# Graph and feed-forward layers on one core: five one-hot rows of each sort group moved to ScalarE

## The chip, the cores and the metric

One core of a Trainium2 chip runs the whole program. The metric is the device time of one execution in microseconds; the number given is the median of three runs. The profile is of a single execution. TensorE multiplies, VectorE, ScalarE and GpSimd do the elementwise work, and DMA queues move data.

## The reference

Four layers, each of a graph network and a feed-forward part, are applied to 384 nodes with 512 features, over 12,288 edges. The change touches the first step of layer 0's graph part only:

```python
def _L0_gnn_ref(x, edges, Wv, bv, Ww, bw, Wa, ba, gamma, beta):
    out = (x @ Wv + bv).reshape(n, H, HD).transpose(1, 0, 2)
    x1, x2 = x[edges[0]], x[edges[1]]
    e = jnp.concatenate([x1, x2], axis=1) @ Ww + bw
    e = e.reshape(-1, H, 2 * HD).transpose(1, 0, 2)
    w = (leaky_relu(e, 0.01) @ Wa + ba)[..., 0]
    mat = full((H, n, n), -inf).at[:, edges[0], edges[1]].set(w)
    y = jnp.matmul(nan_to_num(softmax(mat)), out).transpose(1, 0, 2)
    return layernorm(elu(y).reshape(n, HID) + x) * gamma + beta
...
x = x + _L0_gnn_ref(_layernorm(x), edge_index, ...)
...
x = x + _L3_ffn_ref(_layernorm(x)[None], ...)
```

The kernel multiplies the node features by `Ww` once per node (384 rows instead of 12,288) and gathers the products of an edge's two nodes with one-hot matrices, tile by tile of 128 edges. For that each tile must hold edges of one pair of chunks of 128 nodes, so the edges are sorted into such buckets first.

## The kernel before, in words

The edges lie as 128 partitions x 96 columns (`ET` = 96). For every edge VectorE works out its place in the sorted order, split into a column `q_f` and a row `r_f`, and a key `slo1` that holds both of its node numbers. Sorting is then matrix multiplication: for each of the 96 columns t, a one-hot row matrix `slot_one` (1 where the index equals `q_f[:, t]`) and a matrix `spread` (the key where the index equals `r_f[:, t]`, else 0) are multiplied on TensorE, and all 96 products are summed in the bank `sortk`. Both matrices are 128x128, a "row" of the group in what follows.

The columns go in 12 groups of 8 (`UN`), with two buffers for each kind. A group has 16 such rows. In the kernel before, GpSimd makes 7 of the 8 `slot_one` rows (`POOLED`, line 1153) and VectorE makes the eighth (line 1290) and all 8 spreads (line 1291). Before group g an engine waits on `sort_used` until TensorE has consumed group g-2. TensorE waits for `slot_hot` and `spread_made` of its group.

Between the groups stands other work of TensorE: 12 "units", 128x512 products of the node features with the weights `L0_gnn_Ww`. Four matmuls make a unit; units 6 to 11 have a fifth, the bias row. Units 0 and 1 come first, then

```python
AFTER_GROUP = {1: 2, 2: 3, 4: 4, 5: 5, 7: 6, 8: 7, 10: 8, 11: 9}
SPLIT_AFTER = {0: 0, 1: 1, 3: 2, 4: 3, 6: 4, 7: 5, 9: 6, 10: 7, 11: 8}
```

say behind which group TensorE computes which unit, and behind which group's rows VectorE splits which unit. Units 10 and 11 follow the sort. Each unit u is split into three bf16 parts: ScalarE copies the upper part from PSUM (`top_part`, line 1051), VectorE subtracts it (line 1250), ScalarE copies the middle part (line 1058), and VectorE subtracts again for the lower part (line 1244); it also multiplies and reduces the unit (lines 1253, 1258). In ScalarE's program the copies stand in the order top 0, top 1, middle 0, top 2, middle 1 and so on, and nothing else lies between them in this stage. After group 2's rows VectorE also works out the tiles' chunks (`tile_chunks`).

When `sortk` is full VectorE decodes the keys, TensorE transposes them, and the tile loop over 104 tiles starts once the last unit's parts are made (`parts_made`). GpSimd, when it has made its rows of group 11, writes 20 columns of records to `tab_bucketed` by indirect DMA. The program's order is written out by hand for each engine; there is no scheduler. All of TensorE's matmuls have line 373, a helper's.

Of the kernel before, what the change touches and what calls it, by code (L numbers as in the profile page):

```python
# [11 lines left out]
P = 128  # L12
# [5 lines left out]
ET = E // P  # L18
# [14 lines left out]
UN = 8  # L33
# [129 lines left out]
def gnn_ffn_program(nc, A, out):  # L163
    ctx = ExitStack()
    with ctx:
# [3 lines left out]
        def sem(name):  # L169
            return ctx.enter_context(nc.semaphore(name))  # L170
# [65 lines left out]
        def view(off, *shape):  # L236
            n = 1
            for s in shape:
                n *= s
            assert off + n <= AW, (off, n)  # L240
            v = arena[:, off:off + n]
            if len(shape) == 2:
                v = v.rearrange("p (a b) -> p a b", a=shape[0])
            elif len(shape) == 3:
                v = v.rearrange("p (a b c) -> p a b c", a=shape[0], b=shape[1])
            return v
# [44 lines left out]
        def few_underway(pool, q, earlier, most):  # L291

            if q >= most:
                k = q - most
                pool.wait_ge(ranks_landed[k % UN], 16 * (earlier + k // UN + 1))
        bucketed_loaded = sem("bucketed_loaded")
        bucketed_cleared = sem("bucketed_cleared")
        factor_ready = sem("factor_ready")
# [481 lines left out]
        def flat(a):  # L780
            return a[:].rearrange("p t n -> p (t n)")
# [7 lines left out]
        ew_in = view(tail + 3 * ET, ET)  # L789

        slot5 = ring.slot(5).rearrange("p c n -> p (c n)")
        spread = slot6.rearrange("p (b t r) -> p b t r", b=2, t=UN)
        slot_one = slot7.rearrange("p (b t q) -> p b t q", b=2, t=UN)
        left_f = slot5[:, 0:1024].rearrange("p (b n) -> p b n", b=2)
# [17 lines left out]
        prod_l = slot5[:, 1024:2048].rearrange("p (b h d) -> p b h d", b=2, h=4)  # L812
        s0 = ST * H8
        cs_e, cd_e, slo1, dlo1, q_f, r_f, tmp_e = (xs[:, s0 + k * ET:s0 + (k + 1) * ET] for k in range(7))
        hot9 = flat(cnt_dst)[:, 0:NBK * ET].rearrange("p (k t) -> p k t", k=NBK)
        before9 = flat(mask_dst)[:, 0:NBK * ET].rearrange("p (k t) -> p k t", k=NBK)
        past8 = flat(cnt_dst)[:, 0:ST * 8].rearrange("p (q k) -> p q k", k=8)
# [40 lines left out]
        def unit_part(u, k):  # L858
            r, q, t = UNITS[u]
            return parts0[:, r, t, k, q * 512:q * 512 + 512]  # L860
# [35 lines left out]
        def _(pe, o):  # L896
# [22 lines left out]
            for g in range(ET // UN):  # L919
                pe.wait_ge(slot_hot, g + 1)  # L920
                pe.wait_ge(spread_made, g + 1)
                for j in range(UN):
                    t = UN * g + j
                    last = mm(sk[:, 0:P], slot_one[:, g % 2, j, :], spread[:, g % 2, j, :], t == 0, t == ET - 1)
                last.then_inc(sort_used if g < ET // UN - 1 else banks.full_of("sortk"), 1)
                if g in AFTER_GROUP:
                    if banks.at == sort_bank:
                        banks.at = (sort_bank + 1) % NB
                    unit(AFTER_GROUP[g])
# [114 lines left out]
        @on("act")  # L1044
        def _(act, o):
            act_norm(act, NORM["l0"])
            act_transposed(act, "l0x", xT)

            def top_part(u):
                b = banks.filled(act, unit_name(u))  # L1050
                nc.scalar.activation(unit_part(u, 0), b, ACT.Copy).then_inc(hi_made, 1)

            top_part(0)
            for u in range(len(UNITS)):
                if u + 1 < len(UNITS):
                    top_part(u + 1)
                act.wait_ge(pieces_made, u + 1)
                nc.scalar.activation(unit_part(u, 1), left_f[:, u % 2, :], ACT.Copy).then_inc(bf16_made, 1)
            act.wait_ge(sorted_cleared, 16)

            def eight(i, ahead):
                for b in range(UN):
                    j = b // TB
                    if b % TB == 1 and j < ahead:
                        act.wait_ge(hot_made, 2 * i + j + 2)
                        act.nop(nofuse=True)
                        load_keys(act, 2 * i + j + 3, 1 - j)

                    act.wait_ge(z_free, UN * i + b + 3)
                    for h in range(H8 // 2, H8):  # L1070
                        last = nc.scalar.activation(prod2[:, b % 2, h, :], prod2[:, b % 2, h, :], ACT.Copy, accum_out=w_sum[:, b, h:h + 1])  # L1071
                    last.then_inc(heads_summed, 1)

            act.wait_ge(hot_made, 1)
            load_keys(act, 2)
            FULL = (SB - 3) // 2
            with act.Fori(0, FULL) as i:
                eight(i, 2)
            for i in range(FULL, ST // UN):
                eight(i, min(2, max(0, SB - 3 - 2 * i)))  # L1080

            def head_exp(h, t):
                return nc.scalar.activation(weights_of(h, t), wm[t].rearrange("p (j h) -> p h j", h=H8)[:, h, :], ACT.Exp,
                                            bias=gate[:, 5, t * H8 + h:t * H8 + h + 1])

            def head_transposed(h):
                act_copy(act, f"l0p{h}{NT - 1}", pwT[h % 2][:, NT - 1, :], N)

            nc.scalar.activation(gate[:, 15, 41:42], eps_col[:], ACT.Exp)
            act.wait_ge(neg_max, 1)  # L1090
            for h in range(H8):
                head_exp(h, 0)
            nc.scalar.activation(ost[:, :, :, HD], ones[:, 0:NT * H8].rearrange("p (t h) -> p t h", t=NT), ACT.Copy)
            for t in range(NT):
                b = banks.filled(act, f"l0o{t}")
                nc.scalar.activation(ost[:, t, :, 0:HD], b.rearrange("p (h d) -> p h d", h=H8),
                                     ACT.Copy).then_inc(banks.free_of(f"l0o{t}"), 1)
            act.wait_ge(totals_ready, 1)
            for c in range(NT):
                act_copy(act, f"cnt{c}", cnt_src[:, c, :], N)  # L1100
            act.wait_ge(neg_max, NT)
            for h in range(H8):
                if h >= 2:
                    banks.filled(act, f"l0p{h - 2}{NT - 1}")
                head_exp(h, 1)
                head_exp(h, 2).then_inc(exp_done, 1)
                if h >= 1:
                    if h >= 3:
                        banks.filled(act, f"l0y{h - 3}")
                    head_transposed(h - 1)  # L1110
                if h == 6:
                    elu_part_exp(act, 0)
            banks.filled(act, f"l0y{H8 - 3}")
            head_transposed(H8 - 1)
            elu_part_exp(act, 1)
            elu_part_exp(act, 2)
            act.wait_ge(node_base, 1)
            for c in range(NT):
                act_copy(act, f"cntT{c}", cnt_dst[:, c, :], N)
            for n, (step, t) in enumerate(ROWS0):  # L1120
                act_row_std(act, n, t)
                if step == 3:
                    act.wait_ge(row_ready, 2 * t + 2)
                    nc.scalar.activation(xn2[:, t, :], xn[:, t, :], ACT.Copy, scale=rstd[:, t:t + 1]).then_inc(again_ready, 1)
# [20 lines left out]
        def _(pool, op):  # L1145

            pool.wait_ge(slot_ready, 1)
            for g in range(ET // UN):
                if g >= 2:
                    pool.wait_ge(sort_used, g - 1)  # L1150
                for j in range(POOLED):
                    t = UN * g + j
                    last = nc.gpsimd.tensor_scalar(slot_one[:, g % 2, j, :], iota[:, 0:P], q_f[:, t:t + 1], None, ALU.is_equal)
                last.then_inc(slot_hot, 1)
# [26 lines left out]
        def _(dve, od):  # L1181
# [53 lines left out]
            V.scalar_tensor_tensor(out=pos[:], in0=r_f, scalar=float(ST), in1=q_f, op0=ALU.mult, op1=ALU.add).then_inc(pos_ready, 1)  # L1235

            od.link(V.scalar_tensor_tensor(out=slo1, in0=dlo1, scalar=KEY_BASE, in1=slo1, op0=ALU.mult, op1=ALU.add))
            dve.wait_ge(params, PARAMS)
            wa_bc = wa.unsqueeze(1).broadcast_to([P, 4, P])
            V.tensor_scalar(wa99, wa, 1.0 - 0.01, None, ALU.mult)  # L1240
# [43 lines left out]
            for g in range(ET // UN):  # L1284
                if g >= 2:
                    dve.wait_ge(sort_used, g - 1)
                for j in range(UN):
                    t = UN * g + j
                    if j >= POOLED:
                        V.tensor_scalar(slot_one[:, g % 2, j, :], iota[:, 0:P], q_f[:, t:t + 1], None, ALU.is_equal)  # L1290
                    last = V.tensor_scalar(spread[:, g % 2, j, :], iota[:, 0:P], r_f[:, t:t + 1], slo1[:, t:t + 1],
                                           ALU.is_equal, ALU.mult)
                last.then_inc(spread_made, 1)
                if g == 2:
                    tile_chunks()
                if g in SPLIT_AFTER:
                    split_unit(SPLIT_AFTER[g])
# [1995 lines left out]
```

## Time and profile before

| | us |
|---|---|
| median of 3 runs | 1792.34 |
| lowest and highest run | 1790.09, 1795.05 |
| profiled execution, its own time | 1795.19 |
| its span in the profile | 1793.4 |
| TensorE busy | 1601.0 |
| VectorE busy | 881.6 |
| GpSimd busy | 642.0 |
| ScalarE busy | 501.5 |
| sort stage, first unit to the end of unit 11 | 17.56 to 99.21 |

The span is the time between the profile's first and last event; the execution's own time is slightly longer. "Busy" is the time in which an engine computes. "PEclk" is the clock granted to TensorE as a share of its full 2.4 GHz, so 0.50 is 1.2 GHz. In a timeline a row is one instruction or several like it in a row (xN), and its bracket gives the idle time of the engine just before it and what ended that. Neighbouring instructions on an engine overlap a little, so the distance of starts can be smaller than a duration.

### The profile page before, as it was taken

The numbers are of one execution on the slowest core, as the hardware profiler recorded it, in microseconds if no ns is written. First come the engines' busy times: TensorE is split into PE (matmuls) and PEld (weight loads), VectorE is DVE, ScalarE is ACT, GpSimd is POOL, SyncE is SP. The second block draws the span as 40 slices with busy tenths as digits, with TensorE's granted clock in tenths as the row PEclk, the third lists the DMA queues.
The fourth block names the chain that finished last, engine by engine and source line by source line (L and its number), as shares of the span: only waits on it lengthen the run. The fifth ranks groups of instructions, "written<-read, shape, count | busy, mean of one in ns | idle before, by whom it ended". The sixth has DMA issues, their size and how long they took to land. (4 is left out here: it accounts for less than half of the span.)

```text
span 1793.4 us, 22802 instructions
## 1 busy us (share of the span) xinstructions
PE 1601.0 (89%) x6910; PEld 888.4 (50%) x6940; DVE 881.6 (49%) x2161; ACT 501.5 (28%) x1586; POOL 642.0 (36%) x756
## 2 busy tenths in 40 slices
PE   6989999998697999999996877589799999999798
PEld 3534444446444645555553645334344555555555
DVE  8878888878644343344354154598623101111322
ACT  1134444447431413223231124311200111111234
POOL 5868787873332333333341713556300000000000
PEclk9989999999698999999997887589799999999899
DMA  8030101005413223122316744445326121220020
GB/s 313 2 102 25 60 25 60 25 8 133 124 48 127 78 82 90 57 81 63 94 42 135 255 138 140 138 133 160 118 71 216 51 91 52 99 67 16 9 62 18
DMA packets 119611, 161.71 MB, mean 90 GB/s; under 512 B 49497, under 2 KB 61721, under 8 KB 119154
## 3 DMA queue, kind: packets, MB, share of 16 engines
q1 hardware_dynamic: 93056, 115.43, 20.6%
q0 software_dynamic: 18592, 29.91, 6.1%
q10 hardware_dynamic: 7890, 15.44, 2.6%
q8 instruction: 41, 0.67, 0.2%
q14 instruction: 32, 0.26, 0.1%
HBM read 145.26 MB, written 15.47 MB: 90 GB/s over the span
## 5 line engine op out<-in xcount | busy, mean ns | idle before, releaser
L373 PE MATMUL psum<-arena 128*128 128x384 f32 (+9 forms) x1804 | 319.8, 333 | 33.0 <-issue 13.3
L373 PE MATMUL psum<-arena,ring 128*128 (+1 forms) x1478 | 323.2, 364 | 9.0 <-issue 6.3
L373 PE MATMUL psum<-xT,ring 128*128 128x384 f32 x928 | 317.5, 503 | 10.4 <-ACT ring L3118 4.5
L373 PEld LDWEIGHTS psum<-arena 128*128 128x128 f32 (+5 forms) x1804 | 197.3, 155 | 162.8 <-issue 88.3
L373 PE MATMUL psum<-ring,arena 128*128 128x512 f32 (+1 forms) x570 | 261.9, 607 | 8.6 <-DVE ring L663 3.9
L373 PE MATMUL psum<-ring,xT 128*128 128x512 f32 x552 | 253.9, 613 | 2.1 <-DMA bc<-in_wide 0.8
L373 PEld LDWEIGHTS psum<-xT,ring 128*128 128x128 f32 x928 | 181.5, 197 | 139.9 <-issue 28.3
L373 PEld LDWEIGHTS psum<-arena,ring 128*128 128x128 bf16 (+1 forms) x1504 | 139.7, 115 | 130.3 <-issue 29.0
L1071 ACT ACTIVATE ring<-ring 128x128 f32<-128x128 f32 x416 | 123.3, 297 | 173.6 <-DVE ring L1357 164.6
L373 PEld LDWEIGHTS psum<-ring,xT 128*128 128x128 f32 x552 | 106.0, 197 | 125.4 <-issue 121.6
L373 PEld LDWEIGHTS psum<-ring,arena 128*128 128x128 f32 (+1 forms) x570 | 99.7, 188 | 131.3 <-issue 130.2
L851 POOL DMA_INDIRECT tab_bucketed<-rec,pos x96 | 95.7, 997 | 190.0 <-DMA tab_bucketed<-rec,pos 182.4
L2144 POOL DMA_INDIRECT tab_sorted<-rec,pos x104 | 100.0, 962 | 173.2 <-DMA tab_sorted<-rec,pos 151.1
L1357 DVE SCALAR_TENSOR_TENSOR ring<-psum,wa 128x1024 f32<-128x1024 f32 x104 | 127.3, 1224 | 61.4 <-PE psum L373 60.5
L1165 POOL TENSOR_SCALAR arena<-iota,arena 128x128 bf16<-128x128 f32 x200 | 121.6, 616 | 16.8 <-DVE xT L1371 13.9
L1177 POOL DMA_INDIRECT tab_w<-xT,pair x104 | 109.8, 1056 | 48.8 <-DMA tab_w<-xT,pair 31.9
L408 ACT ACTIVATE arena<-psum 128x384 f32<-128x384 f32 (+1 forms) x130 | 61.9, 498 | 182.8 <-PE psum L373 157.6
L482 ACT ACTIVATE std<-mv,eps_col 128x1 f32<-128x1 f32 x57 | 16.8, 294 | 220.9 <-DVE mv L465 217.9
L1071 ACT ACTIVATION_READ_ACCUMULATOR ring<-ring 128x1 f32 x416 | 77.5, 186 | 0.0
L624 POOL DMA_INDIRECT ring<-tab_h,sd_t x61 | 62.6, 1026 | 37.1 <-issue 13.3
L2071 DVE TENSOR_TENSOR xn<-xn,psum 128x512 f32<-128x512 f32 x24 | 16.5, 687 | 118.7 <-PE psum L373 118.5
L1365 DVE TENSOR_REDUCE mask_dst<-ring 128x4 f32<-128x512 f32 x104 | 70.2, 675 | 0.0
(478 smaller groups left out, 1667.3 us busy)
## 6 DMA issues: line engine op xcount, KB each, us to landing
ring<-in_L_ffn_w SPq DMA_DIRECT2D x22, 1024.0 KB, 6.8
ring<-in_L_gnn_m_w SPq DMA_DIRECT2D x8, 1024.0 KB, 6.0
ring<-in_L_ffn_expert_weights SPq DMA_DIRECT2D x8, 1024.0 KB
ring<-tab_key ACTq DMA_DIRECT2D x24, 256.0 KB
ring<-in_L_gnn_Wv SPq DMA_DIRECT2D x5, 1024.0 KB, 5.1
tab_w<-xn SPq DMA_DIRECT2D x6, 768.0 KB, 14.7
ring<-in_L_gnn_Ww SPq DMA_DIRECT2D x4, 1024.0 KB
ring<-in_L_gnn_wq SPq DMA_DIRECT2D x4, 1024.0 KB
```

The lines of the kernel that those rows point to most:

```text
L373: return nc.tensor.matmul(o, a, b, start=start, stop=stop)
L408: nc.scalar.activation(dst, b[:, 0:w], ACT.Copy).then_inc(banks.free_of(name), 1)
L482: nc.scalar.activation(std[:, t:t + 1], mv[:, t, 1:2], ACT.Sqrt, bias=eps_col[:, 0:1]).then_inc(row_std, 1)
L624: return nc.gpsimd.indirect_dma_start(o, None, table, bass.IndirectOffsetOnAxis(ap=column.bitcast(U32), axis=0), **more)
L851: nc.gpsimd.indirect_dma_start(tab_bucketed, bass.IndirectOffsetOnAxis(ap=pos[:, q:q + 1].bitcast(U32), axis=0), rec[:, q, :], None).then_ ...
L1071: last = nc.scalar.activation(prod2[:, b % 2, h, :], prod2[:, b % 2, h, :], ACT.Copy, accum_out=w_sum[:, b, h:h + 1])
L1165: last = nc.gpsimd.tensor_scalar(edge_is[:, j, k, s_, :], iota[:, 0:P], key_rq[:, s_, T:T + 1], None, ALU.is_equal)
L1177: nc.gpsimd.indirect_dma_start(tab_w, bass.IndirectOffsetOnAxis(ap=pair[:, q:q + 1].bitcast(U32), axis=0), w_edge0[:, q, :], None).then_in ...
L1357: V.scalar_tensor_tensor(out=prod2[:, b % 2], in0=z_bank[:, b % 2], scalar=0.0, in1=wa_all, op0=ALU.max, op1=ALU.mult).then_inc(z_free, 1)
L1365: V.tensor_reduce(w_sum[:, b, 0:H8 // 2], prod2[:, b % 2, 0:H8 // 2, :], AX, ALU.add).then_inc(halves_summed, 1)
L2071: V.tensor_tensor(xn2[:, t, :], xn2[:, t, :], b, ALU.add).then_inc(banks.free_of(f"{tag}{t}"), 1)
L2144: nc.gpsimd.indirect_dma_start(tab_sorted, bass.IndirectOffsetOnAxis(ap=pos2[:, q:q + 1].bitcast(U32), axis=0), rec[:, q, :], None).then_i ...
```

## The change

Of the 16 rows of a group, five move to ScalarE, which makes each in two activations. With `ACT_SLOTS` = 3, GpSimd no longer makes the `slot_one` rows 0 to 2 of a group (4 are left), and with `ACT_SPREADS` = 2, VectorE no longer makes the spreads 0 and 1 (6 are left, and its one slot row). ScalarE first computes the distance |index - place| for the five into a new double buffer `apart`, waits on `apart_made` for its own results, then computes ReLU(1 - distance) for slot rows, and ReLU(key - key x distance) for spreads. VectorE provides `key_less`, the negated key, in one more instruction (`keys_ready`). TensorE waits for one more semaphore a group, `act_hot`. ScalarE's copies of the units keep their order among themselves, and stand behind the groups as in `SPLIT_AFTER`.

```diff
--- before.py
+++ after.py
@@ -293,6 +293,9 @@
             if q >= most:
                 k = q - most
                 pool.wait_ge(ranks_landed[k % UN], 16 * (earlier + k // UN + 1))
+        apart_made = sem("apart_made")
+        act_hot = sem("act_hot")
+        keys_ready = sem("keys_ready")
         bucketed_loaded = sem("bucketed_loaded")
         bucketed_cleared = sem("bucketed_cleared")
         factor_ready = sem("factor_ready")
@@ -789,6 +792,7 @@
         ew_in = view(tail + 3 * ET, ET)
 
         slot5 = ring.slot(5).rearrange("p c n -> p (c n)")
+        ACT_SLOTS, ACT_SPREADS = 3, 2
         spread = slot6.rearrange("p (b t r) -> p b t r", b=2, t=UN)
         slot_one = slot7.rearrange("p (b t q) -> p b t q", b=2, t=UN)
         left_f = slot5[:, 0:1024].rearrange("p (b n) -> p b n", b=2)
@@ -812,6 +816,8 @@
         prod_l = slot5[:, 1024:2048].rearrange("p (b h d) -> p b h d", b=2, h=4)
         s0 = ST * H8
         cs_e, cd_e, slo1, dlo1, q_f, r_f, tmp_e = (xs[:, s0 + k * ET:s0 + (k + 1) * ET] for k in range(7))
+        key_less = cs_e
+        apart = view(e0, 2, ACT_SLOTS + ACT_SPREADS, P)
         hot9 = flat(cnt_dst)[:, 0:NBK * ET].rearrange("p (k t) -> p k t", k=NBK)
         before9 = flat(mask_dst)[:, 0:NBK * ET].rearrange("p (k t) -> p k t", k=NBK)
         past8 = flat(cnt_dst)[:, 0:ST * 8].rearrange("p (q k) -> p q k", k=8)
@@ -919,6 +925,7 @@
             for g in range(ET // UN):
                 pe.wait_ge(slot_hot, g + 1)
                 pe.wait_ge(spread_made, g + 1)
+                pe.wait_ge(act_hot, g + 1)
                 for j in range(UN):
                     t = UN * g + j
                     last = mm(sk[:, 0:P], slot_one[:, g % 2, j, :], spread[:, g % 2, j, :], t == 0, t == ET - 1)
@@ -1050,12 +1057,35 @@
                 b = banks.filled(act, unit_name(u))
                 nc.scalar.activation(unit_part(u, 0), b, ACT.Copy).then_inc(hi_made, 1)
 
-            top_part(0)
-            for u in range(len(UNITS)):
+            def middle_part(u):
                 if u + 1 < len(UNITS):
                     top_part(u + 1)
                 act.wait_ge(pieces_made, u + 1)
                 nc.scalar.activation(unit_part(u, 1), left_f[:, u % 2, :], ACT.Copy).then_inc(bf16_made, 1)
+
+            top_part(0)
+            act.wait_ge(keys_ready, 1)
+            for g in range(ET // UN):
+                if g >= 2:
+                    act.wait_ge(sort_used, g - 1)
+                rows = [(r_f, UN * g + j) for j in range(ACT_SPREADS)] + [(q_f, UN * g + j) for j in range(ACT_SLOTS)]
+                for k, (at, t) in enumerate(rows):
+                    last = nc.scalar.activation(apart[:, g % 2, k, :], iota[:, 0:P], ACT.Abs, bias=at[:, t:t + 1], scale=-1.0)
+                last.then_inc(apart_made, 1)
+                act.wait_ge(apart_made, g + 1)
+                for k, (at, t) in enumerate(rows):
+                    j = t % UN
+                    if k < ACT_SPREADS:
+                        nc.scalar.activation(spread[:, g % 2, j, :], apart[:, g % 2, k, :], ACT.Relu, bias=slo1[:, t:t + 1],
+                                             scale=key_less[:, t:t + 1])
+                    else:
+                        last = nc.scalar.activation(slot_one[:, g % 2, j, :], apart[:, g % 2, k, :], ACT.Relu, bias=ones[:, 0:1],
+                                                    scale=-1.0)
+                last.then_inc(act_hot, 1)
+                if g in SPLIT_AFTER:
+                    middle_part(SPLIT_AFTER[g])
+            for u in range(len(SPLIT_AFTER), len(UNITS)):
+                middle_part(u)
             act.wait_ge(sorted_cleared, 16)
 
             def eight(i, ahead):
@@ -1148,7 +1178,7 @@
             for g in range(ET // UN):
                 if g >= 2:
                     pool.wait_ge(sort_used, g - 1)
-                for j in range(POOLED):
+                for j in range(ACT_SLOTS, POOLED):
                     t = UN * g + j
                     last = nc.gpsimd.tensor_scalar(slot_one[:, g % 2, j, :], iota[:, 0:P], q_f[:, t:t + 1], None, ALU.is_equal)
                 last.then_inc(slot_hot, 1)
@@ -1235,6 +1265,7 @@
             V.scalar_tensor_tensor(out=pos[:], in0=r_f, scalar=float(ST), in1=q_f, op0=ALU.mult, op1=ALU.add).then_inc(pos_ready, 1)
 
             od.link(V.scalar_tensor_tensor(out=slo1, in0=dlo1, scalar=KEY_BASE, in1=slo1, op0=ALU.mult, op1=ALU.add))
+            V.tensor_scalar(key_less, slo1, -1.0, None, ALU.mult).then_inc(keys_ready, 1)
             dve.wait_ge(params, PARAMS)
             wa_bc = wa.unsqueeze(1).broadcast_to([P, 4, P])
             V.tensor_scalar(wa99, wa, 1.0 - 0.01, None, ALU.mult)
@@ -1288,8 +1319,9 @@
                     t = UN * g + j
                     if j >= POOLED:
                         V.tensor_scalar(slot_one[:, g % 2, j, :], iota[:, 0:P], q_f[:, t:t + 1], None, ALU.is_equal)
-                    last = V.tensor_scalar(spread[:, g % 2, j, :], iota[:, 0:P], r_f[:, t:t + 1], slo1[:, t:t + 1],
-                                           ALU.is_equal, ALU.mult)
+                    if j >= ACT_SPREADS:
+                        last = V.tensor_scalar(spread[:, g % 2, j, :], iota[:, 0:P], r_f[:, t:t + 1], slo1[:, t:t + 1],
+                                               ALU.is_equal, ALU.mult)
                 last.then_inc(spread_made, 1)
                 if g == 2:
                     tile_chunks()
```

Line numbers of the changed kernel are some 3 to 32 higher. On ScalarE, from its last copy of the transposed features to the copies that follow group 3, the order was this before the change (`xT`, `arena` and `ring` hold the features, the units' parts and the buffers; line 1051 is the upper part of units 0, 1, 2 and 3, line 1058 the middle part of units 0, 1 and 2):

```order
L408 ACTIVATE xT<-psum 128x384 [waits bank_full3]
L1051 ACTIVATE arena<-psum 128x512 [waits bank_full5]
L1051 ACTIVATE arena<-psum 128x512 [waits bank_full6]
L1058 ACTIVATE arena<-ring 128x512 [waits pieces_made]
L1051 ACTIVATE arena<-psum 128x512 [waits bank_full0]
L1058 ACTIVATE arena<-ring 128x512 [waits pieces_made]
L1051 ACTIVATE arena<-psum 128x512 [waits bank_full1]
L1058 ACTIVATE arena<-ring 128x512 [waits pieces_made]
```

In the changed program it is this, from the rows of group 1 on (line 1073 is the distances, 1079 the spreads, 1082 the slot rows, 1058 and 1064 the upper and middle parts):

```order
L1073 ACTIVATE arena<-iota,xT 128x128 x5
L1079 ACTIVATE ring<-arena,xT 128x128 [waits apart_made]
L1079 ACTIVATE ring<-arena,xT 128x128
L1082 ACTIVATE ring<-arena,ones 128x128 x3
L1058 ACTIVATE arena<-psum 128x512 [waits bank_full0]
L1064 ACTIVATE arena<-ring 128x512 [waits pieces_made]
L1073 ACTIVATE arena<-iota,xT 128x128 [waits sort_used]
L1073 ACTIVATE arena<-iota,xT 128x128 x4
L1079 ACTIVATE ring<-arena,xT 128x128 [waits apart_made]
L1079 ACTIVATE ring<-arena,xT 128x128
L1082 ACTIVATE ring<-arena,ones 128x128 x3
```

Between group 1's rows and group 2's stand the copy of unit 2's upper part, which waits until TensorE has filled its bank (`bank_full0`), and the middle part of unit 1. The same pair stands between groups 3 and 4, 4 and 5, and so on.

TensorE's own order is unchanged. In the changed program its first groups read so; the 128x128 rows are groups 1 to 4, the 128x512 rows units 2 and 3:

```order
L376 MATMUL psum<-ring 128x128 [waits act_hot,spread_made,slot_hot]
L376 MATMUL psum<-ring 128x128 x7
L376 MATMUL psum<-ring,xT 128x512 [waits bank_free0]
L376 MATMUL psum<-ring,xT 128x512 x3
L376 MATMUL psum<-ring 128x128 [waits act_hot,spread_made,slot_hot]
L376 MATMUL psum<-ring 128x128 x7
L376 MATMUL psum<-ring,xT 128x512 [waits bank_free1,slot_arrived1]
L376 MATMUL psum<-ring,xT 128x512 x3
L376 MATMUL psum<-ring 128x128 [waits act_hot,spread_made,slot_hot]
L376 MATMUL psum<-ring 128x128 x7
L376 MATMUL psum<-ring 128x128 [waits act_hot,spread_made,slot_hot]
L376 MATMUL psum<-ring 128x128 x7
```

What is new there is the wait for `act_hot` at the head of each group.

## Rows read from the trace of the kernel before

**Rows 1.** Page: TensorE's busy time, share, instructions; the chain's shares of the span by engine.
```profile
PE 1601.0 (89%) x6910; PEld 888.4 (50%) x6940; DVE 881.6 (49%) x2161; ACT 501.5 (28%) x1586; POOL 642.0 (36%) x756
...
PE 30%; DVE 3%; issue 1%; ACT 1%; DMA 0%; POOL 0%; another core or an unknown queue 0%; ACTq 0%; DVEq 0%
```

**Rows 2.** Windows: length, busy us per engine, PEclk, DMA share, GB/s; sort stage, tile loop.
```profile
40.00:60.00 20.00, 17.34 (x74) 10.88 (x73) 19.46 (x57) 2.23 (x4) 17.79 (x27) 0.91 0.00 1
60.00:80.00 20.00, 20.00 (x105) 13.14 (x105) 18.07 (x50) 3.35 (x6) 16.89 (x30) 1.00 0.00 1
120.00:140.00 20.00, 19.30 (x118) 9.49 (x117) 16.43 (x47) 8.95 (x56) 14.84 (x20) 1.00 0.09 29
```

**Rows 3.** Timeline, TensorE, sort stage: start us, us, instruction [idle before <-releaser].
```profile
27.21 2.05 PE L373 MATMUL psum<-ring 128*128 128x128 f32 x16 [0.26 <-POOL ring L1153]
31.26 2.79 PE L373 MATMUL psum<-ring 128*128 128x128 f32 x16 [1.99 <-POOL ring L1153]
33.84 4.57 PE L373 MATMUL psum<-ring,xT 128*128 128x512 f32 x8
38.24 1.95 PE L373 MATMUL psum<-ring 128*128 128x128 f32 x16
40.03 3.60 PE L373 MATMUL psum<-ring,xT 128*128 128x512 f32 x8
...
48.07 2.50 PE L373 MATMUL psum<-ring 128*128 128x128 f32 x16 [2.65 <-DVE ring L1291]
50.36 4.84 PE L373 MATMUL psum<-ring,xT 128*128 128x512 f32 x8
...
73.83 1.12 PE L373 MATMUL psum<-rows,ones 1*128 1x512 f32 x2
```

**Rows 4.** Timeline of ScalarE, sort stage.
```profile
23.55 0.60 ACT L1051 ACTIVATE arena<-psum 128x512 bf16<-128x512 f32 x1 [9.93 <-PE psum L373]
...
55.24 0.60 ACT L1051 ACTIVATE arena<-psum 128x512 bf16<-128x512 f32 x1 [10.46 <-PE psum L373]
55.73 0.62 ACT L1058 ACTIVATE arena<-ring 128x512 bf16<-128x512 f32 x1
```

**Rows 5.** Timeline of VectorE, sort stage: rows of group 4.
```profile
45.35 1.99 DVE L1291 TENSOR_SCALAR ring<-iota,xT 128x128 f32<-128x128 f32 x7
...
47.46 0.46 DVE L1291 TENSOR_SCALAR ring<-iota,xT 128x128 f32<-128x128 f32 x1
```

**Rows 6.** Timeline of GpSimd, sort stage: rows of groups 0 to 6.
```profile
22.88 32.00 POOL L1153 TENSOR_SCALAR ring<-iota,xT 128x128 f32<-128x128 f32 x49 [18.01 <-DVE xT L1232]
```

**Rows 7.** Groups by form, ScalarE, whole span: busy us, mean ns | idle before.
```profile
L1071 ACT ACTIVATE ring<-ring 128x128 f32<-128x128 f32 x416 | 123.3, 297 | 173.6 <-DVE ring L1357 164.6 <-issue 9.0
...
L408 ACT ACTIVATE arena<-psum 128x384 f32<-128x384 f32 x124 | 58.3, 494 | 170.4 <-PE psum L373 145.2 <-PE psum L2273 20.8 <-PE psum L2281 3.6
...
L1973 ACT ACTIVATE arena<-psum,packed 128x384 f32<-128x384 f32 x48 | 27.8, 580 | 98.8 <-PE psum L373 98.8
...
L1051 ACT ACTIVATE arena<-psum 128x512 bf16<-128x512 f32 x12 | 7.2, 597 | 73.9 <-PE psum L373 73.9
...
L1124 ACT ACTIVATE xn<-xn,rstd 128x512 f32<-128x512 f32 x3 | 2.2, 721 | 3.7 <-DVE rstd L1535 3.7
```

**Rows 8.** Timeline of ScalarE, tile loop.
```profile
112.06 0.29 ACT L1071 ACTIVATE ring<-ring 128x128 f32<-128x128 f32 x1
...
112.26 0.19 ACT L1071 ACTIVATION_READ_ACCUMULATOR ring<-ring 128x1 f32 x1
```

**Rows 9.** Windows, columns as in rows 2: behind two stops, and the tile loop's start.
```profile
33.00:35.00 2.00, 2.00 (x7) 1.48 (x7) 2.00 (x7) 0.00 (x0) 2.00 (x4) 0.50 1.02 427
50.00:52.00 2.00, 2.00 (x5) 1.04 (x5) 2.00 (x7) 0.00 (x0) 2.00 (x5) 0.50 0.00 0
105.00:110.00 5.00, 5.00 (x16) 2.02 (x17) 0.17 (x1) 0.00 (x0) 3.84 (x4) 0.50 0.04 5
110.00:111.00 1.00, 1.00 (x5) 0.41 (x3) 0.51 (x1) 0.00 (x0) 0.00 (x0) 0.56 0.03 2
```

## The prediction

> **What bounds the kernel now.** I read the page first: TensorE is busy in 89% of the span, every other engine in half of it or less, and the chain of waits is TensorE for 30 of the 35% that it covers [rows 1]. The chain does not reach back to the sort stage, so I took that stage from the windows: TensorE computes in 17.34 of 20 us in one and in all 20 of the next, while VectorE works 19.46 and 18.07, GpSimd 17.79 and 16.89 and ScalarE 2.23 and 3.35 [rows 2]. Then I read each engine's timeline there, looking for the starts that have an idle time and a releaser in brackets. From 27 us on, TensorE stands twice: 1.99 us before group 1, for GpSimd, and 2.65 us before group 4, for VectorE [rows 3]. Elsewhere its groups and units follow each other without a gap. So the rows of the one-hot matrices bound the stage only there, 4.6 us in all, and TensorE bounds the rest.
>
> Each of these two stops costs more than its length. A group takes 1.95 us and a unit 3.60 us at full speed; behind the stops they take 2.79 and 4.57, and 2.50 and 4.84 [rows 3]. That is 1.81 us and 1.79 us more. The granted clock in those stretches is 0.50, the 1.2 GHz level, against 1.00, 2.4 GHz, before [rows 9].
>
> ScalarE is idle for most of the stage, but look at what ends its idle times: each of its copies of a unit's upper part starts 0.04 us after TensorE ends that unit (50.36 + 4.84 = 55.20, the copy at 55.24), after 10.46 us of waiting [rows 3, 4]. It is free in time, but it stands at a place in its program.
>
> **What the change removes.** GpSimd makes four rows a group instead of seven, at 32.00 / 49 = 0.65 us each [rows 6]: 2.0 us less. VectorE makes six spreads instead of eight, at 1.99 / 7 = 0.28 us [rows 5]: 0.57 us less. At best this takes away both stops and their slow stretches: 4.6 + 3.6 = 8.2 us. No DMA is added or moved, on no queue.
>
> **What it adds.** VectorE's one more multiplication, over 96 elements, costs no more than a 128-element row at 0.28 us [rows 5] and runs ahead of the first group beside units 0 and 1: nothing on the path. On ScalarE it adds ten activations a group. Their kind is not in the trace; I build it from the nearest rows. A 128x128 ACTIVATE lasts 0.297 us, and the next instruction starts 0.20 us after it did (112.06, 112.26) [rows 7, 8]. A bias column makes 128x384 cost 580 instead of 494 ns, so +0.09; a scale column makes 128x512 cost 721 instead of 597 ns, so +0.12 [rows 7]. Eight activations with a bias column at 0.29, two with both at 0.41, and 0.1 at the end of each half, whose last result is waited for, give 3.3 us a group. The lower bound is copies without columns, 2.2 us; the upper bound ten at 0.41 and as much for the waits, 4.3 us. I take 3.3, since both column costs are seen. The Trainium skill (ScalarE: Activation LUTs, What ACT_TABLE_LOAD costs) prices each pointer operand at about 93 ns; an estimate from that page gives 3.1 us, which would make the sum below 1.6 us smaller.
>
> **What is queued behind what.** This decides. ScalarE's program now runs: rows of group g, then (after groups 0, 1, 3, 4, 6, 7, 9, 10, 11) the copy of the *next* unit's upper part, which waits for TensorE to finish that unit, then the middle part, and only then the rows of group g+1. But TensorE takes the unit after group g and group g+1 directly behind the unit. Where both stand in that order, ScalarE cannot start group g+1 before TensorE has ended the unit, and TensorE then waits for it. One such **link** is: 0.04 us to see the unit's end, 0.49 for the upper copy (55.24 to 55.73) and 0.51 for the middle one (0.62 less an overlap of 0.11) [rows 4], 3.3 for the ten, and 0.15 until TensorE starts (VectorE's row ended at 47.46 + 0.46 = 47.92, group 4 started at 48.07) [rows 3, 5]. Together 4.5 us.
>
> - Groups 2, 5, 8 and 11 come directly behind a unit whose upper part ScalarE must copy first: 4 x 4.5 = 18.0 us.
> - Groups 4, 7 and 10 come one group later, so 1.9 us of the link lies beside a group's matmuls: 3 x 2.6 = 7.8 us.
> - Groups 3, 6 and 9 have their rows made during the group and unit before them: nothing.
> - Groups 0 and 1: ScalarE is free at 23.55 + 0.49 = 24.04 [rows 4], has group 0 at 27.35 and, after unit 1's two copies (1.0 us), group 1 at 31.65. TensorE starts them at 27.5 and 31.8 instead of 27.21 and 31.26: 0.5 us, the stop before group 1 stays.
> - The 2.65 us before group 4 is within the new link: minus 2.65.
>
> Idle time in all: 18.0 + 7.8 + 0.5 - 2.65 = 23.7 us.
>
> **The clock.** Each stop so far brought a slow stretch that costs 1.8 us. The nearest rows for a longer stop are the start of the tile loop: the clock stays at 0.50 during five fully busy us and at 0.56 in the next one [rows 9], nearly 6 us of work at half speed, which cost 2.9, say 3.0 us. For the four long stops I take the middle, 2.4; for the three short ones 1.8; group 4's own 1.8 was there before. 4 x 2.4 + 3 x 1.8 - 1.8 = 13.2 us; the bounds are 10.8 (all at 1.8) and 19.2 (all at 3.0).
>
> **Where it ends.** VectorE and GpSimd wait for these groups too and only shift. The tile loop is TensorE's (19.30 of 20 us busy [rows 2]), so nothing behind the sort takes the delay up. Sum: 23.7 + 13.2 = 36.9 us. The profiled execution took 1795.19 us and would take 1832; the median of the three runs, 1792.34, lies 2.85 us lower, and I forecast against it: 1829 us. Ends: with 2.2 us a group and the clock's lower bound, links of 3.4 us give 4 x 3.4 + 3 x 1.5 - 2.65 and 0.9 us won before group 1, 14.5 + 10.8 = 25 us, so 1818. With 4.3 us and the upper bound, links of 5.5 give 4 x 5.5 + 3 x 3.6 - 2.65 + 2.5 lost before group 1, 32.7 + 19.2 = 52 us, so 1844.
>
> **Rivals.**
>
> - *The gain arrives* (the other side): ScalarE's rows are ready before TensorE comes to each group, and both old stops and slow stretches go, -8.2 us: 1784. For it: ScalarE works only 2 to 3 of 20 us [rows 2]. Against it: this needs ScalarE to make a group's rows before TensorE ends the unit ahead of it, and in its order the copy that waits for that unit stands first. It decides at one point: if group 2's first activation starts before unit 2 ends. 4%.
> - *No further slow stretches*: stops as worked out, but the clock does not fall again: +23.7, 1816. Against it: both stops of 2.0 and 2.65 us brought one. 5%.
> - *The clock never recovers between the stops*: from group 2 to unit 9 all work runs at the lower level. That is 10 groups x 1.9, 3 units x 3.6 and 4 units with a bias row (1.12 more, overlapping, [rows 3]) x 4.65, 48.4 us, doubled; less 1.8 that was there, and 5.7 because groups 3, 6 and 9 then hide all but 0.7 of each short link: +64.6, 1857. For it: stops now come every 6 to 9 us and the loop's first 5 us stayed slow. Against it: behind the old stops the clock was back within the same unit. 4%. The Trainium skill (TensorE: Matmul & The Clock Gate, HAM oscillation) tells of a kernel where every burst of matmuls behind a wait runs at the low clock; by that rule this rival would hold. The rows of the two old stops do not bear it out for bursts as long as a group and a unit, the loop's row is closer to it.
> - *No effect*: the delay is taken up before the tile loop, by work that was late anyway: 1792. Nothing in the stage waits for anything but these engines. 3%.
>
> **How the numbers follow.** The forecast has 84%, its own ends are 1818 and 1844. From 1816 to 1842 the range takes in the rival without slow stretches and leaves out the top of the forecast, the slow rival and the two at or below the old time, about 15%. A measurement of this kernel can tell about 0.3%, some 5 us, from no change. Faster: the first rival, 4%. The same: 3%. Slower: 93%.
>
> **What would show it.** In the changed profile ScalarE's first activation of group 2 starts about 1.0 us after unit 2's end, and TensorE's idle time before groups 2, 5, 8 and 11 is 4.5 us each and before 4, 7 and 10 2.6 us each, all released by ScalarE. ScalarE's ten activations span 3.3 us. The granted clock shows a stretch of 0.50 behind each. The tile loop begins near 142 us instead of 104.97. If TensorE's idle time there stays near 5 us, the reading of the order is wrong; if it is 24 us and the total differs, the clock term is.

## The result, and the profile after

| | before | with the change |
|---|---|---|
| median, us | 1791.21 (4 runs) | 1824.48 (4 runs) |
| lowest and highest run | 1789.6, 1795.05 | 1823.06, 1827.87 |
| profiled execution | 1795.19 | 1824.89 |
| first matmul of the tile loop | 104.97 | 138.77 |

The change makes the kernel slower: the ratio of the times, new to old, is 1.0192, 95% interval 1.0179 to 1.0204, 33.3 us in the medians. The forecast was 1829 us, in a range from 1816 to 1842. One of the old kernel's 19 executions beside the last three experiments took 4204.76 us and is left out of their ratios.

The page's lines on busy times and on the chain (TensorE's busy time was 1601.0 us [rows 1]):

```profile
PE 1607.4 (88%) x6910; PEld 892.3 (49%) x6940; DVE 875.5 (48%) x2138; ACT 539.4 (30%) x1706; POOL 625.8 (34%) x720
...
PE 80%; DVE 8%; ACT 4%; issue 3%; DMA 2%; POOL 2%; ACTq 0%; another core or an unknown queue 0%; DVEq 0%; POOLq 0%
```

TensorE is busy 6.4 us longer over the whole span with the same 6910 matmuls, and its share falls. The chain now reaches back to the start and is not comparable in its shares with the one of before.

TensorE's timeline in the sort stage, groups (x16, 128x128) and units (x8, 128x512), the idle time before each in brackets; the last row is the tile loop's first matmul:

```profile
27.66 2.02 PE L376 MATMUL psum<-ring 128*128 128x128 f32 x16 [1.17 <-ACT ring L1082]
31.90 2.02 PE L376 MATMUL psum<-ring 128*128 128x128 f32 x16 [2.23 <-ACT ring L1082]
33.76 3.60 PE L376 MATMUL psum<-ring,xT 128*128 128x512 f32 x8
41.90 3.43 PE L376 MATMUL psum<-ring 128*128 128x128 f32 x16 [4.54 <-ACT ring L1082]
45.17 3.60 PE L376 MATMUL psum<-ring,xT 128*128 128x512 f32 x8
...
53.31 2.02 PE L376 MATMUL psum<-ring 128*128 128x128 f32 x16 [2.75 <-ACT ring L1082]
55.17 3.60 PE L376 MATMUL psum<-ring,xT 128*128 128x512 f32 x8
63.30 3.75 PE L376 MATMUL psum<-ring 128*128 128x128 f32 x16 [4.54 <-ACT ring L1082]
66.85 4.54 PE L376 MATMUL psum<-ring,xT 128*128 128x512 f32 x8
...
75.93 3.48 PE L376 MATMUL psum<-ring 128*128 128x128 f32 x16 [2.75 <-ACT ring L1082]
...
88.43 3.75 PE L376 MATMUL psum<-ring 128*128 128x128 f32 x16 [4.54 <-ACT ring L1082]
91.97 3.93 PE L376 MATMUL psum<-ring,xT 128*128 128x512 f32 x8
...
101.50 2.50 PE L376 MATMUL psum<-ring 128*128 128x128 f32 x16 [2.56 <-POOL ring L1183]
103.79 4.85 PE L376 MATMUL psum<-ring,xT 128*128 128x512 f32 x8
...
114.22 3.75 PE L376 MATMUL psum<-ring 128*128 128x128 f32 x16 [4.54 <-ACT ring L1082]
117.77 4.68 PE L376 MATMUL psum<-ring,xT 128*128 128x512 f32 x8
...
138.77 1.03 PE L376 MATMUL psum<-arena,ring 128*128 x2 [2.05 <-DVE gate L1372]
```

Compare [rows 3]. TensorE now waits before groups 2, 5, 8 and 11 for 4.54 us each and before groups 4, 7 and 10 for 2.75, 2.75 and 2.56 us. Before groups 0 and 1 it is 1.17 and 2.23 us. That is 29.6 us in all, against 4.9 before. Behind six of these seven stops the group or its unit is slow: a group takes up to 3.75 us instead of 1.95. Behind group 4's stop both run at full speed.

ScalarE's timeline between unit 2 and group 2:

```profile
37.40 0.60 ACT L1058 ACTIVATE arena<-psum 128x512 bf16<-128x512 f32 x1 [5.64 <-PE psum L376]
37.89 0.62 ACT L1064 ACTIVATE arena<-ring 128x512 bf16<-128x512 f32 x1
38.41 1.56 ACT L1073 ACTIVATE arena<-iota,xT 128x128 f32<-128x128 f32 x5
40.00 0.88 ACT L1079 ACTIVATE ring<-arena,xT 128x128 f32<-128x128 f32 x2
40.79 0.97 ACT L1082 ACTIVATE ring<-arena,ones 128x128 f32<-128x128 f32 x3
```

Here is the link, piece by piece. Unit 2 ended at 33.76 + 3.60 = 37.36, and the copy of its upper part starts at 37.40; the middle copy follows at 37.89; the five distances start only at 38.41; the last slot row ends at 41.76, and TensorE's group 2 starts at 41.90. That is 4.54 us, none of which was on the path before.

The three groups of ScalarE's new activations (columns: busy us, mean ns | idle before):

```profile
L1073 ACT ACTIVATE arena<-iota,xT 128x128 f32<-128x128 f32 x60 | 18.7, 389 | 0.5 <-DVE xT L1268 0.5
L1082 ACT ACTIVATE ring<-arena,ones 128x128 f32<-128x128 f32 x36 | 11.6, 386 | 0.0
L1079 ACT ACTIVATE ring<-arena,xT 128x128 f32<-128x128 f32 x24 | 10.5, 486 | 0.4
```

Idle and busy time of TensorE from group 0 to the last unit, before and after, by the windows (length, then the busy times of TensorE, its weight loads, VectorE, ScalarE and GpSimd, then TensorE's granted clock, DMA share and GB/s; both windows reach 0.8 to 1.0 us past the last unit):

```profile
27.00:100.00 73.00, 67.35 (x286) 40.21 (x286) 64.75 (x173) 11.88 (x22) 59.79 (x90) 0.95 0.27 102
```

```profile
27.00:134.00 107.00, 76.94 (x286) 47.97 (x286) 56.61 (x150) 47.78 (x134) 46.56 (x63) 0.86 0.21 77
```

The stretch is 107 instead of 73 us. TensorE is idle in 30.1 instead of 5.7 us of it, and its busy time for the same 286 matmuls is 76.9 instead of 67.4 us, at a mean granted clock of 0.86 instead of 0.95. So of 34.0 us more, 24.4 are waiting and 9.6 are the same work done more slowly.

### The profile page after: what moved, and what is told of

It is laid out like the page before. It is cut to its first block, busy times and chain, and to the rows that moved or that the text cites. A ratio compares the mean times of both kernels' runs of the same rounds, so it can differ in the third digit from the quotient of the medians.

```text
span 1822.9 us, 22862 instructions
## 1 busy us (share of the span) xinstructions
PE 1607.4 (88%) x6910; PEld 892.3 (49%) x6940; DVE 875.5 (48%) x2138; ACT 539.4 (30%) x1706; POOL 625.8 (34%) x720
## 4 chain that ended last, share of the span: by engine, by line
PE 80%; DVE 8%; ACT 4%; issue 3%; DMA 2%; POOL 2%; ACTq 0%; another core or an unknown queue 0%; DVEq 0%; POOLq 0%
PE psum L376 79%; DVE stats L467 1%; DMA ring<-tab_h,sd_t 1%; POOL ring L627 1%; ACT arena L1073 1%; PE psum L1027 1%; DVE xn L2084 0%; ACT ring L1082 0%; ACT ring L1079 0%; DVE xn L2090 0%; DVE xn L2103 0%; DMA arena<-tab_x 0%; DVE arena L2691 0%; DVE mv L468 0%; DMA x<-in_x 0%
## 5 line engine op out<-in xcount | busy, mean ns | idle before, releaser
L376 PE MATMUL psum<-arena 128*128 128x384 f32 (+9 forms) x1804 | 315.7, 329 | 21.4 <-DVE arena L666 6.3
L1207 POOL DMA_INDIRECT tab_w<-xT,pair x104 | 110.1, 1058 | 48.0 <-DMA tab_w<-xT,pair 32.1
L376 PE MATMUL psum<-ring 128*128 128x128 f32 (+1 forms) x404 | 68.9, 292 | 30.2 <-ACT ring L1082 27.1
L485 ACT ACTIVATE std<-mv,eps_col 128x1 f32<-128x1 f32 x57 | 16.8, 294 | 220.8 <-DVE mv L468 217.8
```

Source lines behind the costliest of these rows:

```text
L376: return nc.tensor.matmul(o, a, b, start=start, stop=stop)
L1207: nc.gpsimd.indirect_dma_start(tab_w, bass.IndirectOffsetOnAxis(ap=pair[:, q:q + 1].bitcast(U32), axis=0), w_edge0[:, q, :], None).then_in ...
```

## The experiments

**Theory 1** is the prediction's: the order on ScalarE costs the time. The copy of a unit's upper part, which must wait for that unit, stands before the rows that TensorE needs right behind it. **Theory 2**: two activations a row are too much work for ScalarE, or disturb the other engines, wherever they stand. A second question is the size of the clock's share.

All kernels of the experiments, but not the old kernel that they are compared with, check against their bounds two values that SyncE loads in layer 0. The control is the changed kernel with this and nothing else (arguments cut at `...`):

```diff
-sp.wait_ge(w_landed, nc.values_load(landings[0:1, t:t + 1], ..., min_val=16, max_val=16 * ST, skip_runtime_bounds_check_because=...))
+sp.wait_ge(w_landed, nc.values_load(landings[0:1, t:t + 1], ..., min_val=16, max_val=16 * ST))
```

> The changed kernel as it is, but the two values that SyncE loads and waits against in layer 0 are checked against their bounds when they are loaded. All kernels of this study carry that check, so this one is what they are compared with. Every theory: 1824 us, within 3.

Measured: 1828.26 us (1827.25 to 1829.49), ratio to before 1.0224 (1.02 to 1.0248). That is 3.8 us above the changed kernel's own median, and 1.3 us above the end of what was expected. Its stops from group 1 on have the same lengths, 2.23, 4.54, 2.75 and 2.56 us. The difference arises early. Unit 0 starts at 18.89 instead of 17.80, released by the parameters' DMA; units 0 and 1 take 10.14 instead of 8.68 us, of which a shorter stop before group 0 (0.59 instead of 1.17 us) takes back 0.6. And group 1 is followed by a slow stretch that the changed kernel's profile does not have:

```profile
33.87 2.54 PE L376 MATMUL psum<-ring 128*128 128x128 f32 x16 [2.23 <-ACT ring L1082]
36.20 4.81 PE L376 MATMUL psum<-ring,xT 128*128 128x512 f32 x8
```

Compare 2.02 and 3.60 there: 1.7 us, at the same stop of 2.23 us. Together that is 3.7 of the 4.0 us by which the tile loop starts later (142.77 instead of 138.77). These 3.7 us lie before the check: SyncE runs its instructions at 136.3 and again at 250.5 us, 0.2 us in all each time. From the tile loop's start to the end the control's profile took 1683.5 us and the changed kernel's 1684.1. So the two profiles show no cost of the check, though one profile of each does not exclude a small one. Experiments are compared with this control, and where they are compared with the old kernel, the check counts against them.

**Rows ahead of the copies.** The same activations, in another place:

```diff
-            for g in range(ET // UN):
+            def act_rows(g):
...
+            act_rows(0)
+            for g in range(ET // UN):
+                if g + 1 < ET // UN:
+                    act_rows(g + 1)
                 if g in SPLIT_AFTER:
                     middle_part(SPLIT_AFTER[g])
```

> Same 120 activations of ScalarE, same rows on every engine, but ScalarE makes the rows of group g+1 before the copies that stand behind group g. Theory 1 (the order: a copy that waits for a unit stands before rows that TensorE needs next): the four stops of 4.54 us and the three of 2.7 us vanish, with their slow stretches; at most the stop before group 4 stays, since VectorE's tile_chunks stands before group 3's rows. 1786 to 1793 us. Theory 2 (ScalarE's two activations a row are simply too much work, or slow the other engines): the stops stay for the most part, over 1810 us.

Measured: 1789.27 us, ratio to before 0.9997 (0.9986 to 1.0009; the old kernel's median beside these experiments was 1789.50), 39 us below the control. TensorE's timeline, the groups 0, 1, 2, 4, 7 and unit 4:

```profile
28.47 2.02 PE L376 MATMUL psum<-ring 128*128 128x128 f32 x16 [0.59 <-ACT ring L1082]
31.72 2.02 PE L376 MATMUL psum<-ring 128*128 128x128 f32 x16 [1.23 <-ACT ring L1082]
...
37.02 1.95 PE L376 MATMUL psum<-ring 128*128 128x128 f32 x16
...
46.95 3.51 PE L376 MATMUL psum<-ring 128*128 128x128 f32 x16 [2.47 <-DVE ring L1328]
50.26 3.79 PE L376 MATMUL psum<-ring,xT 128*128 128x512 f32 x8
...
61.84 2.02 PE L376 MATMUL psum<-ring 128*128 128x128 f32 x16 [0.78 <-ACT ring L1082]
```

Group 2 follows its unit without idle time, and so do 5, 8, 10 and 11. All that is left is 0.59, 1.23 and 0.78 us for ScalarE, and 2.47 us before group 4, for VectorE. With the same 120 activations on ScalarE the loss is gone, so theory 2 falls. The stop before group 4 is VectorE's:

```profile
36.48 1.01 DVE L1306 TENSOR_TENSOR cnt_dst<-iota,gate 128x832 f32<-128x832 f32 x1
...
40.50 1.41 DVE L1328 TENSOR_SCALAR ring<-iota,xT 128x128 f32<-128x128 f32 x5
...
44.80 1.48 DVE L1328 TENSOR_SCALAR ring<-iota,xT 128x128 f32<-128x128 f32 x5
```

From 36.48 to 40.50 it works out the tiles' chunks, and only then makes group 3's rows, splits a unit and makes group 4's (44.80).

**Two rows on ScalarE.** The order of the change, a smaller dose:

```diff
-        ACT_SLOTS, ACT_SPREADS = 3, 2
+        ACT_SLOTS, ACT_SPREADS = 1, 1
```

> One slot row and one spread on ScalarE instead of three and two; GpSimd makes six, VectorE seven. The order is that of the change. Theory 1: a link is 1.0 us of copies, 1.5 us of four activations and 0.2 us of signals, 2.7 us instead of 4.54, so the four long stops are 2.7 us and the three short ones 0.9 us: some 13 us less idle time, and fewer slow stretches, 1803 to 1811 us. If only the copies' wait counted and not the rows' own length, it would stay at 1824.

Measured: 1799.92 us (1796.98 to 1802.58), ratio 1.0064 (1.0039 to 1.0089), 28.3 us below the control and 3 us below the lower end of what was expected. Group 2, unit 3, groups 4 and 5:

```profile
39.28 2.43 PE L376 MATMUL psum<-ring 128*128 128x128 f32 x16 [2.69 <-ACT ring L1082]
41.51 4.91 PE L376 MATMUL psum<-ring,xT 128*128 128x512 f32 x8
...
49.12 2.02 PE L376 MATMUL psum<-ring 128*128 128x128 f32 x16 [0.91 <-ACT ring L1082]
...
57.27 3.27 PE L376 MATMUL psum<-ring 128*128 128x128 f32 x16 [2.69 <-ACT ring L1082]
```

The stops have the expected lengths, 2.69 us for the long ones, 0.91, 0.91 and 0.71 for the short ones. With four activations a link is 2.69 us and with ten 4.54, so one activation adds 0.31 us, and some 1.45 us would be left without any: the copies and the signals. The stops of 0.91 us bring no slow stretch. The total came out lower than expected because of a part that these rows do not touch. Against the changed kernel's profile the tile loop starts 18.0 us earlier (120.74 instead of 138.77), which by itself would give 1807 us, inside what was expected. The other 6.4 us lie behind the tile loop's start, 1677.7 us in this profile and 1684.1 in that one (the last section).

**Filled waits.** To take the clock's share apart from the waiting, TensorE multiplies zeros into the sort bank while it would wait:

```diff
             for g in range(ET // UN):
+                for _ in range({2: 14, 5: 14, 8: 14, 11: 14, 4: 8, 7: 8, 10: 8}.get(g, 0)):
+                    mm(sk[:, 0:P], zeros[:, 0:P], zeros[:, 0:P], False, False)
                 pe.wait_ge(slot_hot, g + 1)
```

> The changed kernel with matmuls of zeros into the sort bank before each group that TensorE waits for: 14 before groups 2, 5, 8 and 11 (about 3.5 us), 8 before groups 4, 7 and 10 (about 2 us). They add nothing to the sums and lie in time in which TensorE waited. Theory 1 with a clock term: the granted clock stays at 1.00 in the sort stage, units and groups take 3.60 and 1.95 us, and 9 to 12 us come back: 1812 to 1816. If the slow stretches cost nothing beside the waits: 1824 or a little more.

Measured: 1811.42 us (1809.91 to 1812.42), ratio 1.0126 (1.0103 to 1.015), 16.8 us below the control, though TensorE waits for the same rows. That is 0.6 us below the range that was expected. The zeros before group 5, the group and its unit; then the windows of the stage with filled waits and, for comparison, of the control:

```profile
61.62 3.29 PE L376 MATMUL psum<-zeros 128*128 128x128 f32 x28
66.32 2.02 PE L376 MATMUL psum<-ring 128*128 128x128 f32 x16 [1.42 <-ACT ring L1084]
68.18 3.60 PE L376 MATMUL psum<-ring,xT 128*128 128x512 f32 x8
```

```profile
41.00:124.00 83.00, 75.03 (x406) 51.17 (x404) 42.18 (x110) 42.14 (x118) 36.00 (x48) 1.00 0.08 24
```

```profile
45.00:137.00 92.00, 69.78 (x246) 43.14 (x246) 40.83 (x107) 38.22 (x108) 39.51 (x52) 0.83 0.12 40
```

The group takes 2.02 instead of 3.75 us, the unit 3.60 instead of 4.64. The clock stays at 1.00, the 2.4 GHz level, against a mean of 0.83. The stage is shorter by the slow work alone: the tile loop starts at 131.24 instead of 142.77, 11.5 us earlier, while unit 0 started 0.87 us later, so 12.4 us. By these profiles 4.0 us more lie behind the tile loop's start, where nothing was changed (the last section), so of the 16.8 us in the medians only the 12.4 are shown to be the clock's. So the slow clock of that stage is a cost of its own, and TensorE need not do anything useful to avoid it.

**What is to be gained.** The stop before group 4 could be taken away directly. Three kernels move `tile_chunks`:

```diff
-                if g == 2:
+                if g == 8:
                     tile_chunks()
```

These three ran on another chip, where the old kernel's median was 1789.54 us. First with the rows ahead:

> ScalarE's rows ahead of its copies, and VectorE's tile_chunks behind group 8's rows instead of group 2's. With the rows ahead one stop was left that VectorE ended, 2.47 us before group 4, with a slow stretch behind it. If tile_chunks (4.3 us on VectorE) causes it, both go: 4 us below the kernel with the rows ahead, 1785 us, 0.2% faster than the old kernel. If VectorE's steady work is the bound, the stop only moves: 1789 us.

Measured: 1785.61 us, ratio 0.9971 (0.9959 to 0.9983). The groups that TensorE waits for:

```profile
27.74 2.02 PE L376 MATMUL psum<-ring 128*128 128x128 f32 x16 [0.87 <-ACT ring L1082]
30.99 2.02 PE L376 MATMUL psum<-ring 128*128 128x128 f32 x16 [1.23 <-ACT ring L1082]
...
44.24 2.02 PE L376 MATMUL psum<-ring 128*128 128x128 f32 x16 [0.78 <-ACT ring L1082]
...
57.48 2.02 PE L376 MATMUL psum<-ring 128*128 128x128 f32 x16 [0.78 <-ACT ring L1082]
```

The stop before group 4 is 0.78 us and ScalarE's, no longer VectorE's: the chunks caused it. No group has a slow stretch. Then the old kernel, without any row on ScalarE:

> The old kernel, rows on GpSimd and VectorE alone, with tile_chunks behind group 8's rows. If the stop of 2.65 us before group 4 comes from tile_chunks: TensorE waits only before group 1 (1.99 us, for GpSimd), 4 us less than the old kernel, 1785 to 1786 us, so that ScalarE's help is worth no more than the stop before group 1. If GpSimd's 7 rows a group then bound the first groups, the stop before group 4 stays at 1 us or more and the gain is under 3 us.

Measured: 1786.44 us, ratio 0.9983 (0.9974 to 0.9992). Groups 1, 4 and 7:

```profile
31.52 2.05 PE L373 MATMUL psum<-ring 128*128 128x128 f32 x16 [1.74 <-POOL ring L1153]
...
44.55 2.05 PE L373 MATMUL psum<-ring 128*128 128x128 f32 x16 [0.54 <-POOL ring L1153]
...
58.03 2.05 PE L373 MATMUL psum<-ring 128*128 128x128 f32 x16 [0.99 <-POOL ring L1153]
```

The stop before group 4 fell from 2.65 to 0.54 us and is GpSimd's, and its slow stretch is gone. Neither of the two outcomes that were expected came whole: the gain is 3.1 us, and small stops for GpSimd stay before groups 4 and 7. The three stops for GpSimd make 3.3 us (0.17 us for VectorE before group 9 is all else): this is what moving rows to ScalarE can still take out of this profile. The profile also lacks the slow stretch behind group 1 (2.05 and 3.60 us, where the old kernel's profile has 2.79 and 4.57). That place lies ahead of the moved work, behind a stop of 1.74 instead of 1.99 us. How much of the 3.1 us in the medians belongs to it, and how much to the chunks, is not shown. At last three rows on ScalarE (`ACT_SLOTS, ACT_SPREADS = 2, 1`), made ahead, with the chunks late:

> As the kernel with the rows ahead and tile_chunks late, but only two slot rows and one spread on ScalarE. Its six activations are 2 us, so it no longer holds up groups 0 and 1 (0.59 and 1.23 us with the rows ahead) nor group 7 (0.78 us): TensorE's idle time in the sort stage is under 1 us, 1 to 2 us below the kernel with five rows: 1783 to 1784 us. If GpSimd's five rows a group bind instead: as with five rows.

Measured: 1782.98 us (1781.75 to 1783.57), ratio 0.996 (0.9946 to 0.9974): faster than the old kernel by 6.6 us, 0.4%, and than the old kernel with the chunks late by 3.5 us. From group 0 on to the last unit one idle time is left, and the tile loop starts 7.2 us earlier than before:

```profile
30.30 2.02 PE L376 MATMUL psum<-ring 128*128 128x128 f32 x16 [0.37 <-issue]
...
97.77 1.03 PE L376 MATMUL psum<-arena,ring 128*128 x2 [1.84 <-DVE gate L1377]
```

## Why the prediction was right

- **The place.** The prediction rested on ScalarE's order: the copy of unit u+1's upper part stands before the rows of the group behind that unit. All seven stops are where it put them, ScalarE ends six, and GpSimd, 0.02 us later than ScalarE, the seventh. The experiment that only changes this order takes the loss away.
- **The link.** 4.5 us was forecast, 4.54 measured; for the short stops 2.6, and 2.75, 2.75 and 2.56 measured. Groups 3, 6 and 9 wait for nothing, as worked out. The activations were priced from the nearest rows at 0.29 and 0.41 us from start to start; ten took 3.35 us against 3.3. The Trainium skill (ScalarE: Activation LUTs, What ACT_TABLE_LOAD costs) gives 93 ns for each pointer operand: the trace agrees, with 297 ns for a 128x128 ACTIVATE without such an operand [rows 7], 389 with one and 486 with two.
- **Idle time.** 23.7 us more was forecast, 24.7 measured. Most of the 1 us lies in groups 0 and 1: 3.4 us of stops where 2.8 was implied; the short stops add 0.3 and the long ones 0.2.
- **The clock** is the term that was mis-sized: 13.2 us forecast, 9.0 found by adding what groups and units took over 1.95 and 3.60 us (12.6 after, 3.6 before), 9.6 by the windows. The four long stops cost 1.5, 2.7, 2.1 and 2.9 us, 2.3 on average, where 2.4 was taken. The three short ones cost 0, 1.5 and 1.8 us where each was given 1.8: that step took every stop of 2 us or more to bring a slow stretch, since both old ones had, and so forecast a stretch of 0.50 behind each. The stop before group 1 was even longer than before, 2.23 against 1.99 us, and its slow stretch went. These errors, 0.4 for the long stops, 2.1 for the short ones and 1.8 for group 1, are the 4.2 us by which the term was too large.
- **The total.** For the profiled execution 1832 us was forecast and 1824.89 came. 4.2 us are the clock and 1.0 us of idle time lies on the other side, so the tile loop starts at 138.77 where near 142 was forecast. Another 4.3 us lie behind its start: from there to the end of the span it took 1688.4 us before and 1684.1 after. The change does nothing there, so more than half of the distance has nothing to do with the mechanism. The old kernel's profile is of an execution 4 us above its median.
- **The rivals.** *The gain arrives* fell at its own point: group 2's first activation started 1.05 us after unit 2's end, not before it. With the order repaired the two old stops did not both go either: the one before group 4 was VectorE's chunks, so in the order tried half of the 8.2 us stayed, and what took it away was another change, to VectorE's program. *No further slow stretches* and *the clock never recovers* both fell: it fell six times and came back each time before the next stop. For the latter the Trainium skill (TensorE: Matmul & The Clock Gate, HAM oscillation) tells of a kernel where every burst behind a wait starts slow. So did every group behind a long stop here, at a granted clock of 0.50, but the work that followed was back at 1.00 within the group or its unit (from 45 us on behind group 2, from 69, 93 and 120 behind groups 5, 8 and 11).

## What to carry to other kernels

An idle engine is only free from the place in its program at which the new work stands: look at what the instruction ahead of that place waits for, and whether the engine that waits for the new work is the one that it waits for. Here the same 120 activations cost 39 us or nothing, by their place among 24 copies of another kind. And before work is moved to relieve an engine, name what is late at each stop: one of the two stops was a detour of 4.3 us in VectorE's program, and the old kernel with that alone moved was 3.1 us faster, of the 6.6 us that the best kernel gained.

## What the runs showed beside this

- A stop's length did not tell whether a slow stretch follows. At 2.23 us before group 1 one did in the control and with filled waits, and none in the changed kernel; at 2.75 us, in the changed kernel and the control alike, none behind group 4's stop and one behind group 7's. At 2.69 us, with two rows on ScalarE, one did four times of four, at 4.54 us one always did, and at 1.74 us (the old kernel with the chunks late) and under, before a group, none did. Matmuls of zeros kept the clock at 1.00.
- The unchanged part behind the tile loop's start varies. In the profiled executions it took 1688.4 us (before), 1684.1 (the change), 1683.5 (control), 1682.1 (rows ahead), 1679.5 (filled waits), 1677.7 (two rows) and, with the chunks late, 1684.3, 1682.7 and 1682.7. Of the 4.3 us between the old and the changed kernel 4.1 arise in one stretch: the first 4092 matmuls behind the tile loop's start take 951.0 us in both, the next lasts 319.0 us before (1056.00 to 1375.00, granted clock 0.83) and 314.9 after (1089.80 to 1404.70, 0.86), and the rest 418.4 and 418.2. TensorE is busy 1.1 us less there and idle 3.0 us less. Why is open; no experiment was made on it. These differences bound what one profile's total can tell; the stage is therefore compared by its own start and end here.
- The start of unit 0 lay between 17.56 and 19.76 us in these profiles, each time behind the DMA of the wide parameters.
